# Four GpSimd residual sums per first-layer unit, each made as three sums of one token tile

## What is computed

```python
h = concatenate([edges(x), text_embedding(x_txt)], axis=1)      # 8 x 384 x 256
n = layernorm(h)
a = n + attention(layernorm(n)) @ Wo + bo                        # 16 heads of 16
h = h + a + gelu(layernorm(a) @ W1 + b1) @ W2 + b2
h = h + relu(layernorm(h) @ ternary(f1) + bf1) @ ternary(f2) + bf2
h = h + attention2(layernorm(h)) @ Wo1                           # 16 heads of 64, ALiBi
h = h + mixture_of_experts(layernorm(h))                         # 8 experts, top 2
```

## Time and profile before

| | |
|---|---|
| median of 3 runs | 1863.71 us (1862.79 to 1864.31) |
| profiled execution, its own time | 1864.7 us |
| its span | 1862.9 us |
| PE busy | 1720.3 us (92%) |
| DVE busy | 1255.3 us (67%) |
| ACT busy | 970.3 us (52%) |
| POOL busy | 693.1 us (37%) |

### The profile page before, as it was taken

How to read it: one execution, slowest core, us unless ns; L and a number is a source line. 1 busy time by engine, 2 the same in 40 slices (tenths; PEclk the granted TensorE clock), 3 DMA queues, 4 the chain that set the end, 5 groups by cost and what they waited for, 6 DMA issues and landing times.

```text
span 1862.9 us, 33716 instructions
## 1 busy us (share of the span) xinstructions
PE 1720.3 (92%) x11231; PEld 1413.5 (76%) x11231; DVE 1255.3 (67%) x4074; ACT 970.3 (52%) x2670; POOL 693.1 (37%) x1084
## 2 busy tenths in 40 slices
PE   4687999999999999899999999974999999999997
PEld 3465777777767677678887788853898999899896
DVE  6578778787778675858777878767755445444542
ACT  1356657575667667656667777620334333333421
POOL 2251434324242421433444445430534524533431
PEclk8688999999999999999999999985899999999998
DMA  7112010101011010101011110021232321122210
GB/s 215 40 38 66 1 64 3 62 10 55 10 38 60 2 35 2 35 23 48 27 35 35 35 35 27 2 80 33 92 102 66 109 91 62 39 81 68 65 41 22
DMA packets 74245, 91.04 MB, mean 49 GB/s; under 512 B 16523, under 2 KB 64310, under 8 KB 74072
## 3 DMA queue, kind: packets, MB, share of 16 engines
q1 hardware_dynamic: 61464, 67.90, 11.2%
q0 software_dynamic: 9472, 16.77, 3.2%
q10 hardware_dynamic: 3136, 4.21, 0.7%
HBM read 71.02 MB, written 25.00 MB: 52 GB/s over the span
## 4 chain that ended last, share of the span: by engine, by line
PE 65%; issue 13%; DVE 8%; POOL 5%; POOLq 3%; ACT 2%; DVEq 1%; DMA 1%; SPq 0%; ACTq 0%
PE bank L1618 17%; PE bank L1049 12%; PE bank L1633 10%; PE bank L997 6%; PE bank L979 6%; PE bank L1032 5%; PE bank L1214 3%; PE bank L1076 2%; DVE probs L2322 1%; POOLq L3190 1%; POOL rot L3216 1%; POOL rstd_b L3191 1%; ACT probs L1746 1%; DVE at_least L2963 1%; POOLq L3213 1%
## 5 line engine op out<-in xcount | busy, mean ns | idle before, releaser
L1746 ACT ACTIVATE probs<-probs,nmax 128x128 f32<-128x128 f32 (+2 forms) x768 | 381.0, 500 | 64.3 <-DVE nmax L2322 62.8
L997 PE MATMUL bank<-cst,probs 128*128 128x128 f32 x1536 | 237.4, 284 | 20.7 <-ACT probsT L1754 9.9
L3254 POOL TENSOR_SCALAR probs<-probs,rowsum 128x128 f32<-128x128 f32 (+2 forms) x384 | 179.1, 486 | 194.9 <-DVE rowsum L2338 194.7
L997 PEld LDWEIGHTS bank<-cst,probs 128*128 128x128 f32 x1536 | 177.4, 144 | 65.7 <-issue 27.1
L1618 PE MATMUL bank<-xeT,gate_w 128*128 128x480 f32 x768 | 187.7, 380 | 0.5 <-issue 0.5
L1618 PE MATMUL bank<-xeT,up_w 128*128 128x480 f32 x768 | 187.3, 380 | 0.0
L3126 DVE TENSOR_TENSOR prod<-bank,sil 128x480 f32<-128x480 f32 x128 | 84.1, 657 | 147.9 <-PE bank L1618 147.0
L1633 PE MATMUL bank<-down_w,hT 128*120 128x256 f32 x1536 | 181.3, 280 | 0.0
L1633 PEld LDWEIGHTS bank<-down_w,hT 128*120 128x120 f32 x1536 | 179.9, 182 | 0.1
L1754 ACT COPY probsT<-bank 128x384 f32<-128x384 f32 x256 | 120.8, 472 | 105.2 <-PE bank L997 90.6
L2470 DVE COPY probsT<-bank 128x384 f32<-128x384 f32 x256 | 141.6, 553 | 40.6 <-PE bank L997 35.8
(11 more groups left out here) (363 smaller groups left out, 3566.3 us busy)
## 6 DMA issues: line engine op xcount, KB each, us to landing
gate_raw<-in_L_ffn_gate_w SPq DMA_DIRECT2D x8, 1024.0 KB, 4.8
up_raw<-in_L_ffn_up_w SPq DMA_DIRECT2D x8, 1024.0 KB, 6.9
down_raw<-in_L_ffn_down_w SPq DMA_DIRECT2D x8, 1024.0 KB, 5.7
img<-in_x SPq DMA_DIRECT2D x8, 768.0 KB, 5.1
residual_rows<-x SPq DMA_DIRECT2D x8, 384.0 KB, 2.5
residual_rows<-h_in SPq DMA_DIRECT2D x8, 384.0 KB, 3.6
xr<-residual_rows SPq DMA_DIRECT2D x8, 384.0 KB, 4.6
hr<-residual_rows SPq DMA_DIRECT2D x8, 384.0 KB, 3.9
```

The costliest lines, as they stand in the source:

```text
L997: last = tr(ps[bank][:, P * q:P * (q + 1)], probs[:, n % 4, SEG[t] + P * j:SEG[t] + P * (j + 1)], ident)
L1746: last = f(p, p, ACT.Exp, bias=nmax[:, n % 4, t:t + 1], scale=-1.0, accum_out=rowsum[:, where, t:t + 1])
L3254: last = g.tensor_scalar(p, p, rowsum[:, n, t:t + 1], 1.0, ALU.mult, ALU.mult)
```

## The change

Each of the four sums is made as three instructions of 256 columns, one per token tile, and the last of the three carries the semaphore's increment. The order of GpSimd's work, the waits in front of each sum and all other engines' programs stay as they are. The sums ahead of the first unit (`residuals`, L3205 and L3206) stay whole.

```diff
+                def by_tiles(dst, src, bias_row):
+                    for t in range(NT):
+                        last = g.tensor_tensor(dst[:, t, :], src[:, t, :], bias_row, ALU.add)
+                    return last
+
                 def residual_x():
                     if k.conv:
                         pool.wait_ge(norm_ready[LN_ATTN0], at(img_c, NT, NT))
-                        g.tensor_tensor(x1[:], x1[:], row(bo_r), ALU.add).then_inc(resid_made, 1)
+                        by_tiles(x1, x1, bo_r).then_inc(resid_made, 1)
 
                 def residual_h():
                     if k.conv:
-                        g.tensor_tensor(h_in[:], h_in[:], row(b2_r), ALU.add).then_inc(resid_made, 1)
+                        by_tiles(h_in, h_in, b2_r).then_inc(resid_made, 1)
 
                 def mlp_residual():
                     if k.s2:
                         pool.wait_ge(resid_loaded, at(s2_img, 16, 16))
-                        g.tensor_tensor(hr[:], hr[:], xr[:], ALU.add).then_inc(resid2_ready, 1)
+                        for t in range(NT):
+                            last = g.tensor_tensor(hr[:, t, :], hr[:, t, :], xr[:, t, :], ALU.add)
+                        last.then_inc(resid2_ready, 1)
 
                 def ffn_residual():
                     if k.s2:
                         then()
                         pool.wait_ge(norm_ready[LN_MLP], at(s2_img, NT, NT))
-                        g.tensor_tensor(xr[:], hr[:], row(bf2_r), ALU.add).then_inc(resid3_ready, 1)
+                        by_tiles(xr, hr, bf2_r).then_inc(resid3_ready, 1)
```

## The result

The changed kernel took 1853.24 us (median of 4 runs, 1852.73 to 1854.06) against 1864.01 before; the ratio is 0.9938, with a 95% interval of 0.9918 to 0.9958. Forecast were 1856.6 us and 1853.5 to 1862. Another set of runs gave 1854.31 us and a ratio of 0.9954 (0.9936 to 0.9972), so the size of the gain is known to some 3 us only. (Each ratio is to runs of the kernel before made beside it, whose medians were 1863.3 to 1864.6 in the later sets.

What follows compares the result with a forecast made beforehand. U_MID0 units were taken as bound by TensorE, winnable only where it waited. 5.4 us (x_parts) plus 1.7 (relu) made 7.1, from 1863.7 to 1856.6 us; own range 1854.5 to 1858.7, 8 in 10 range 1853.5 to 1862.

Steps and rivals of the forecast that it cites:

- What bounds the kernel, and the port: U_MID0 units: TensorE busy 83.04 of 85.7 us; its waits come from VectorE instructions held until a GpSimd sum ends.
- The cost on GpSimd: Each whole sum cut into three pieces costs GpSimd +0.28 us, 8 us over the run, beside a TensorE not waiting.
- The deviation behind xr: GpSimd's deviation for `attn_norm(2)`, queued behind the xr sum, moves to 406.95; VectorE wants it at 407.07, slack 0.12 us.
- The x_parts term: Five U_MID0 units: normalisation ends 1.08 us earlier, TensorE's wait for `x_parts` falls from 1.42 to 0.34; 5.4 us.
- The relu term: Four U_MID0 units, not the first: `hidden(0)` no longer held by the h_in sum, TensorE's 0.43 us wait goes; 1.7 us.
- A: GpSimd keeps the port through all three pieces, so VectorE is released 0.28 us later: 3.6 us slower, 1867.3; chance 0.10.
- B: Late deviation for `attn_norm(2)` or h_in pieces stopping VectorE take back half the gain: 3.5 us left, 1860.2; chance 0.16.
- C: Earlier VectorE also removes TensorE waits for transposed probabilities, 0.44 us each: 11.0 us gained, 1852.7; chance 0.07.

## Why the prediction was wrong

The direction and the port were right; the gain was put too low, and mainly by one step: a wait of TensorE was priced at its own length, with nothing for the clock behind it. Step by step:

- **What bounds the kernel, and the port.** Right. TensorE's waits for `x_parts` and `relu` were the ones to win, and both came from a VectorE instruction held by a GpSimd sum. Shown by the two orders of a short and a long piece, where only the length of the first counts.
- **The cost on GpSimd.** +0.28 a sum forecast. Three pieces of `x1` take 2.12 where the sum took 1.84: right. Over the run GpSimd's busy time grew by 10.9 us and not 8, since pieces that meet VectorE get longer too. The deviation behind xr ends at 403.25 and VectorE uses it at 403.50: it is not late.
- **The x_parts term**, 5 x 1.08. Right in four units (0.34 left, as worked out). In the first unit the whole wait went, by 0.1 us of issue order. That was luck, and it did not add up to more: the feed-forward matmuls behind `relu` came 0.1 us later there than in the third unit, and the unit is 0.1 longer than its neighbours.
- **The relu term**, 4 x 0.43. The place is right; the size is 0.49 to 0.52 a unit, of which 0.27 is the cut of h_in and the rest most likely that of x1, which had been costed at nothing. The count of four was wrong: the first unit has the `relu` wait too, and the row that seemed to say otherwise (0.55 at 239.93) came from a unit slowed by the clock. Measured are four times 1.60 and 1.47 in the first unit (85.65 to 84.18, both without a dip), 7.9 us for the port instead of 7.1.
- **The term that was put at nothing: TensorE's clock.** This is the step that failed. The prediction has the unit bound by TensorE "at full clock", from one unit, and did not read the window of the first U_MID0. That one has 0.98, and windows of 1 us there show the lower level behind the very wait that the change removes. 6 dips behind 24 waits at 1.24 us on average make 5 x 6/24 x 1.24 = 1.6 us a run, to be had with the 7.9: 9.5 us, an estimate from the traces.
- **What is left.** The medians differ by 10.8 and 10.3 us, the ratios say 11.6 and 8.6, and their intervals (7.8 to 15.3, and 5.2 to 11.9) hold 9.5. A gain of 9.5 alone would give 1854.2, inside the range. The other 1.3 us of the first comparison is within the scatter of whole runs, and nothing here resolves it; that the time fell just outside the range, and not just inside, is chance.
- **The rest of the profiled difference** (1.40 ahead of the eighth mark, 1.6 in the experts, +0.46 at the start) is in all likelihood not of the change. The changed kernel's second execution has 507.9 in the experts, as the kernel before has. The stretch to the eighth mark took 97.09, 97.48 and 97.52 in the kernel before, 96.08 and 96.30 in the changed one, but 96.08 with h_in only and 99.07 with xr only. This is argued from the scatter and not shown by an experiment of its own.
- **The rivals.** A is refuted. B (half of the gain taken back) did not come about, though the run with xr behind h_in shows its mechanism: there it costs 0.5 a unit. C was right in its size and wrong in its cause: more did come free, but not the waits for `probsT`.
- **The range.** Its lower end rested on the port alone. A wait of 1.4 us was priced at 1.4; with the clock it costs 0.3 more on average, and over twice its length in the dearest case seen (2.49 on top).

## What to carry to other kernels

Where VectorE and GpSimd share work, look for VectorE instructions whose duration ends 0.1 to 0.4 us after a GpSimd instruction's: they were held, no view of waits shows it, and cutting GpSimd's instruction (or moving it into an idle time of VectorE's port work) frees them, at 0.14 us of GpSimd per extra instruction, or 0.2 where pieces meet VectorE (10.9 us for 56 of them). A unit that was slowed by the clock is no sample of the others: waits that are missing in it may be there in an undisturbed one. Price an idle time of TensorE with the clock behind it: read the granted clock in windows of 1 or 2 us behind every wait that a change adds or removes, in more than one execution. Then judge changes of this size by the length of a repeated unit, not by the whole run.

## What was not expected of the hardware

- The clock fell behind 6 of 24 idle times of 1.4 us, 4 of 5 of 1.7 to 2.3 us, and never in 40 cases with 0.9 us or less (or no idle time at all), all in the same place of the same loop. Each of the six dips cost 0.9 to 2.5 us, some two thirds of the wait itself or more.
- Which engine gets the port was decided by 0.1 us of issue order (231.60 against 231.73, and 232.35 against 232.23), and it turned a wait of 1.43 us into none, though the unit as a whole gained nothing by it.
- VectorE got in between two queued GpSimd instructions in each case seen, with instructions of 128, 256 and 512 columns; in none of the fourteen traces was a VectorE sum, cast or normalisation held for longer than one GpSimd instruction.
